# Merging the second combine into the first expert stretch of a fused attention and two-mixture kernel

## What is computed

```python
y = x + attention(rmsnorm(x) * scale1)            # linear attention, 16 heads, chunks of 64
z = y + moe(rmsnorm(y) * scale2)                  # 8 experts, top 2, gelu, capacity 1280 rows each
x = layernorm(x + z)                              # the second combine, see below
x = layernorm(x + ffn(layernorm(x) * gamma + beta))   # 8 experts, top 2, silu(g) * u, capacity 1280
```

## Time and profile before

| | us |
|---|---|
| median of three runs | 1545.46 |
| the profiled execution | 1548.21 |
| its span, first to last instruction | 1546.3 |
| PE busy | 1461.0 (94%) |
| DVE busy | 1011.2 (65%) |
| ACT busy | 727.1 (47%) |
| POOL busy | 746.5 (48%) |
| mean granted clock of PE | 0.963 of full |

### The profile page before, as it was taken

One profiled execution on the slowest core, in us unless ns is written; L12 is line 12 of the kernel. 1 busy time (PEld: TensorE's weight loads), 2 busy tenths in 40 slices (PEclk: granted clock), 3 DMA queues, 4 the chain that ended last, 5 costly groups with the idle time before them and its releaser, 6 DMA issues. The chain is left out here.

```text
span 1546.3 us, 36023 instructions
## 1 busy us (share of the span) xinstructions
PE 1461.0 (94%) x11755; PEld 1419.0 (92%) x11755; DVE 1011.2 (65%) x2768; ACT 727.1 (47%) x1735; POOL 746.5 (48%) x749
## 2 busy tenths in 40 slices
PE   8999984999999999999949999999999999999993
PEld 7888864999999999999938999999999999999993
DVE  6999976667667667666565656565565655566455
ACT  4767653555455445545543334343433433344333
POOL 3677652566566566655523344433444334433433
PEclk9999995999999999999968999999999999999996
DMA  7122123244234243342613132413132131411117
GB/s 257 42 70 56 56 73 108 58 102 103 42 96 102 48 96 93 51 130 35 192 50 109 27 111 33 116 29 109 28 108 42 27 109 29 115 34 28 28 24 228
DMA packets 64547, 123.41 MB, mean 80 GB/s; under 512 B 14304, under 2 KB 52832, under 8 KB 61792
## 3 DMA queue, kind: packets, MB, share of 16 engines
q0 software_dynamic: 36416, 46.58, 18.4%
q1 hardware_dynamic: 28064, 76.02, 13.7%
HBM read 79.66 MB, written 42.90 MB: 79 GB/s over the span
## 5 line engine op out<-in xcount | busy, mean ns | idle before, releaser
L972 POOL DMA_INDIRECT acc<-ysb,IDX x160 | 258.8, 1617 | 132.4 <-ACT ysb L1074 66.3
L1111 DVE TENSOR_TENSOR E_hraw<-E_sg,bank 128x256 f32<-128x256 f32 x320 | 134.5, 420 | 282.7 <-ACT E_sg L1042 214.2
L965 POOL DMA_INDIRECT E_mg<-meta,IDX x160 | 151.0, 943 | 335.6 <-DVE E_gate L1095 308.4
L1166 PE MATMUL bank<-E_xT,ws 128*128 128x256 f32 x960 | 272.2, 284 | 5.1 <-DVE E_xT L1086 5.0
L1167 PE MATMUL bank<-E_xT,ws 128*128 128x256 f32 x960 | 271.5, 283 | 0.0
L1168 PE MATMUL bank<-E_xT,ws 128*128 128x256 f32 x960 | 271.3, 283 | 0.0
L1122 DVE TENSOR_TENSOR E_hT<-E_hraw,E_hT 128x256 fp32r<-128x256 f32 x640 | 259.9, 416 | 0.0
L1118 DVE CAST E_hT<-E_hraw 128x256 fp32r<-128x256 f32 x640 | 208.0, 325 | 62.1 <-ACT E_hraw L1045 40.2
L1042 ACT ACTIVATE E_sg<-bank 128x256 f32<-128x256 f32 x320 | 121.6, 384 | 256.3 <-PE bank L1168 243.4
L1166 PEld LDWEIGHTS bank<-E_xT,ws 128*128 128x128 f32 x960 | 183.0, 191 | 6.3 <-issue 5.8
L1166 PE MATMUL bank<-ws,E_hT 128*128 128x256 f32 x640 | 183.8, 287 | 0.0
(11 more groups left out here) (207 smaller groups left out, 3940.6 us busy)
## 6 DMA issues: line engine op xcount, KB each, us to landing
wraw<-in_w_ffn SPq DMA_DIRECT2D x8, 3072.0 KB, 10.7
wraw<-in_w_moe SPq DMA_DIRECT2D x8, 2048.0 KB, 13.0
X<-acc SPq DMA_DIRECT2D x16, 512.0 KB, 5.4
acc<-x SPq DMA_DIRECT2D x32, 128.0 KB, 1.7
xn<-xn SPq DMA_DIRECT2D x32, 128.0 KB, 1.7
acc<-X POOLq DMA_DIRECT2D x4, 1024.0 KB, 8.3
acc<-X SPq DMA_DIRECT2D x8, 512.0 KB, 2.7
out<-C_xo SPq DMA_DIRECT2D x8, 512.0 KB, 5.6
```

Of the source, the lines that this page charges most:

```text
L965: nc.gpsimd.indirect_dma_start(out=mg[:, j, :], out_offset=None, in_=meta_dram, in_offset=at_slots(u, j)).then_inc(s_gm, 16)
L972: nc.gpsimd.indirect_dma_start(out=acc_dram, out_offset=at_slots(u, j), in_=ysb[:, j, :], in_offset=None, compute_op=ALU.add).then_inc(s_y ...
L1111: V.tensor_tensor(hraw[:, f % RING, :], sg[:, f % RING, :], bank[f % RING][:, UW:2 * UW], ALU.mult).then_inc(s_hm, 1)
L1166: nc.tensor.matmul(out, wh, mh, start=first, stop=False)
```

## The change

The combine of stage 4 becomes the tail of E1's block, and the routing a block of its own. In detail:

- The 20 spare products at E1's end go. PE turns the eight early tiles as soon as the last unit's bias add is done, then issues three spare products, then goes on with tile 8. One spare product per tile stays, as before.
- Group 2 is loaded in three pieces: tile 8, tile 9, tiles 10 and 11 (`SPANS`).
- POOL normalises, and SP stores, groups 0 to 5 in the first block; groups 6 and 7 (`LATE` = 2) follow in the routing's block, behind the routing's two constants on POOL.
- ACT's warm-up of the root, which held its table load, goes. The turned tiles go into `b2`, which has the same eight places of 256 columns as `aT` had. `META` moves to a buffer of the whole program.

```diff
@@ SPANS
+SPANS = [(g * G, (g + 1) * G) for g in range(HEAD)] + [(8, 9), (9, 10), (10, 12)]     # HEAD * G = 8
+SPANS += [(g * G, (g + 1) * G) for g in range(HEAD + 1, GROUPS)]
@@ expert_phase, tail=C for E1
             for g in range(HEAD):
                 ...
+            if tail:
+                sp.wait_ge(s_ys, 16 * UT * UNITS)
+                tail.sync(sp)
...
+            if tail:
+                tail.pool(pool, range(GROUPS - LATE))
...
+            if tail:
+                tail.act(act, b2)
...
+            if tail:
+                tail.vector(dve)
...
-            if not glu:
-                keep_busy(nc, bank[7], ws[0], 20)
+            if tail:
+                pe.wait_ge(s_sg, UNITS * NF + RING)
+                pe.wait_ge(s_ye, UNITS * UT + UT)
+                tail.tensor(pe, b2)
@@ class Between, from between_phase; vector() as it was
+    def aT(self, b2, n):
+        return b2[:, n % (2 * G), :].rearrange("p (k t) -> p k t", k=KD)
+    def store(self, sp, groups):
+        for g in groups:
+            t = slice(g * G, (g + 1) * G)
+            sp.wait_ge(self.s_x2, (g + 1) * G)
+            sp.dma_start(by_partition(self.io["acc2"])[:, t, :], self.X[:, t, :]).then_inc(self.s_sa, 16)
+    def sync(self, sp):
+        for i in range(HEAD, len(SPANS)):
+            t = slice(*SPANS[i])
+            sp.dma_start(self.X[:, t, :], by_partition(self.io["acc1"])[:, t, :]).then_inc(self.s_ldx[i], 16)
+        self.store(sp, range(GROUPS - LATE))
...
-            nc.scalar.activation(warm[:, :], eps, ACT.Sqrt)
...
         for n in range(NT + 3):
+            if n == HEAD * G:
+                keep_busy(nc, self.bank[7], self.ws0, 3)
             if n < NT:
                 turn(n)
             keep_busy(nc, self.bank[7], self.ws0, 1)
             if n >= 3:
                 logits(n - 3)
@@ second_routing_phase, a block of its own
+            C.store(sp, range(GROUPS - LATE, GROUPS))
             R.store(sp)
+            sp.wait_ge(C.s_sa, 16 * GROUPS)
...
             R.constants(pool)
+            C.pool(pool, range(GROUPS - LATE, GROUPS))
```

More of the change, by code:

```diff
@@ L1224, in sem @@
             return ctx.enter_context(nc.semaphore(f"C1_{name}"))
[L1226 to L1237, removed]
@@ new lines, in __init__ @@
+        self.wrg, self.fold, self.ws0 = wrg, fold, ws0
+        self.bias = sb("bias", [P, NT, E])
+        self.st = sb("st", [P, 2, G, 6])
+        self.mv = sb("mv", [P, 2, G, 2])
+        self.sd = sb("sd", [P, 2, G, 2])
+        self.rs = sb("rs", [P, NT])
+        self.nb = sb("nb", [P, NT])
+        self.s_ldx = s_head + [sem(f"ldx{g}") for g in range(HEAD, len(SPANS))]
+        self.s_bs, self.s_mv, self.s_sd, self.s_rs, self.s_nb = map(sem, ("bs", "mv", "sd", "rs", "nb"))
+        self.s_x2, self.s_tr, self.s_aT, self.s_rt, self.s_sa, self.s_base = map(sem, ("x2", "tr", "aT", "rt", "sa", "base"))
@@ new lines, in sync, with pool @@
+    def sync(self, sp):
[3 more added lines that the diff above has]
+        self.store(sp, range(GROUPS - LATE))
+    def pool(self, pool, groups):
+        X, rs, nb = self.X, self.rs, self.nb
+        for g in groups:
+            pool.wait_ge(self.s_nb, g + 1)
+            for n in range(g * G, (g + 1) * G):
+                pool.wait_ge(self.s_tr, n + 1)
+                self.nc.gpsimd.tensor_scalar(X[:, n, :], X[:, n, :], rs[:, n:n + 1], nb[:, n:n + 1], ALU.mult, ALU.add).then_inc(self.s_x2, 1)
@@ new lines, in act @@
+    def act(self, act, b2):
+        nc, sd, mv = self.nc, self.sd, self.mv
+        eps, eps2 = self.cst[:, C_EPS:C_EPS + 1], self.cst[:, C_EPS + 1:C_EPS + 2]
+        for g in range(GROUPS):
+            if g >= 2:
+                act.wait_ge(self.s_rt, (g - 1) * G)
+            for n in range(g * G, (g + 1) * G):
+                act.wait_ge(self.s_tr, n + 1)
+                nc.scalar.activation(self.aT(b2, n), self.turned(n), ACT.Copy).then_inc(self.s_aT, 1)
+            act.wait_ge(self.s_mv, (g + 1) * G)
+            if g >= 2:
+                act.wait_ge(self.s_rs, 2 * (g - 1))
+            nc.scalar.activation(sd[:, g % 2, :, 0], mv[:, g % 2, :, 1], ACT.Sqrt, bias=eps).then_inc(self.s_sd, 1)
+            nc.scalar.activation(sd[:, g % 2, :, 1], mv[:, g % 2, :, 1], ACT.Sqrt, bias=eps2, scale=1.0 + EPS).then_inc(self.s_sd, 1)
@@ new lines, in tensor, with turn, logits @@
+    def tensor(self, pe, b2):
+        nc, ident = self.nc, self.cst[:, C_ID:C_ID + P]
+        def turn(n):
+            self.loaded(pe, n)
+            if n >= 5:
+                pe.wait_ge(self.s_aT, n - 4)
+            for k in range(KD):
+                ins = nc.tensor.transpose(self.turned(n)[:, k, :], self.X[:, n, k * P:(k + 1) * P], ident)
+            ins.then_inc(self.s_tr, 1)
+        def logits(n):
+            pe.wait_ge(self.s_aT, n + 1)
+            for k in range(KD):
+                ins = nc.tensor.matmul(self.bank[0][:, D + n * E:D + (n + 1) * E], self.aT(b2, n)[:, k, :], self.wrg[:, k, :],
+                                       start=(k == 0), stop=(k == KD - 1))
+            ins.then_inc(self.s_rt, 1)
+        for n in range(NT + 3):
+            if n == HEAD * G:
+                keep_busy(nc, self.bank[7], self.ws0, 3)
+            if n < NT:
+                turn(n)
+            keep_busy(nc, self.bank[7], self.ws0, 1)
+            if n >= 3:
+                logits(n - 3)
@@ L1296, in _ @@
         def _(dve):
[L1297 to L1328, removed]
-            V.tensor_tensor(bias[:, :, :], bias[:, :, :], fold[:, 0, :].unsqueeze(1).to_broadcast([P, NT, E]), ALU.add).then_inc(s_base, 1)
-            dve.wait_ge(s_base, 2)
-            dve.wait_ge(s_rt, NT)
             R.select(dve)
```

113 lines of the change are left out of this document (50 added, 63 removed).

## The result

The changed kernel took 1537.94 us in the median of five runs (1535.95 to 1541.09), the kernel before 1545.46; the ratio is 0.9959, 95% interval 0.9948 to 0.9970, so 6.3 us less (4.6 to 8.0); the two medians lie 7.5 apart. Forecast were 1543.6 and a range down to 1541.8, with 0.19 for a gain of over 0.2%. The sign was right, but the gain was three times that forecast, and outside the range.

What follows compares the result with a forecast made beforehand. PE was taken to bound the combine's end, with routing waiting for it and the loads for POOL's last add. Terms -2.9 + 0.3 + 0.7 = -1.9 us from 1545.46 gave 1543.6, range 1541.8 to 1546.1.

Steps and rivals of the forecast that it cites:

- Early tiles: Start of the combine: PE goes from the last product to tile 0 at 745.4, 4.4 us earlier than before.
- ACT's table load at nothing: Early tiles of the combine: ACT's 1.28 us table load for the root, after four evictions, costs nothing.
- The load of tile 8 is what is late next, -2.9: Combine: tile 8's 128 KB load takes 2.6 us, so PE turns it at 752.55 instead of 755.46.
- The meeting of the engines, +0.3: Between last logits and first routing operation: the engines' meeting, hidden before, now lies on the path, +0.3 us.
- POOL's last two groups in the routing, +0.7: Routing: POOL working beside DVE slows DVE's operations on two SBUF tensors, +0.7 us.
- The clock falls: Combine loop, rival: PE's idle waits halve its clock, making it slower, about 1563 us; chance 0.05.
- The step that failed: Closing sum over the combine and routing: -1.9 us in all, with the turned tiles' move of memory changing no wait.

Runs made afterwards that it cites:

- e7: The changed kernel with LATE = 0, so that POOL normalises all eight groups before the routing; 1542.95 us in one execution.
- e8: The changed kernel without the three spare products ahead of tile 8; 1560.24 us.
- e1: The kernel before with two unused buffers giving the expert stages' large buffers the change's addresses, nothing else changed; 1544.01 us, ratio 0.9970 to the kernel before.
- e2: The changed kernel with META2 and the combine's buffers at SBUF's other end, so expert buffers keep their old addresses; 1544.13 us, ratio 0.9974 to the kernel before.
- e3: The changed kernel itself, run again word for word on another chip; 1543.29 us, ratio 0.9964 to the kernel before.
- e4: The changed kernel with weights and rows all shifted alike by 32 bytes per partition; 1543.91 us, ratio 0.9968 to the kernel before.
- e5: The changed kernel with the experts' rows and hidden values 64 bytes further from the weights; 1537.72 us in one execution.
- e12: The changed kernel with tiles 8 to 11 loaded in one piece of 512 KB; 1537.63 us in one run.

## Why the prediction was wrong

- **Early tiles**: right. Tile 0 was due 0.7 us ahead of the last add and came at 0.72.
- **ACT's table load at nothing**: right, no wait of PE on an eviction; the load took the 1.28 us of the earlier trace rows.
- **The load of tile 8 is what is late next, -2.9**: right in kind; 2.37 us from issue (746.92) to turn (749.29) where 2.6 + 0.05 were put: -3.1. It starts 3.90 us after the add was issued, forecast 3.79. Over all ten profiles with this piece, issue to turn took 2.36 to 2.81 us, so the forecast size was right and the first profile is at its lower end. The estimate by the Trainium skill (DMA: Bandwidth & Descriptors, Anatomy of one DMA), 2.3 us for 128 KB, is that lower end; the page has its formula from transfers issued by GpSimd, while SyncE issued this one.
- **The meeting of the engines, +0.3**: 772.42 - 771.97 = 0.45 after the last logits, against 0.10 before; +0.35.
- **POOL's last two groups in the routing, +0.7**: e7 gives 0.75. Of it only 0.4 is new, since the kernel before paid the first part already (0.54 beside POOL), which I did not take off. The Trainium skill (GPSIMD Engine Reference, Specifications) has GpSimd contend with VectorE's operations that read two SBUF inputs, or that run in a two-port mode. The trace agrees for the first: products of two SBUF tensors took up to 0.66 for 0.42, and reductions stayed at 0.42. The one-input clamp at 773.36 was stretched too, 0.38 against 0.29 in e7; whether it is of the second kind no run here shows.
- R_sel to IDX 0.34 shorter, in every kernel with the merged block. Not forecast; VectorE no longer stands idle for 0.25 us there; the cause is open.
- **The clock falls**, 0.05: it did not, and e8 shows that it was a real branch with the right price. The forecast wait of 0.75 us was 0.42, and up to 0.71 in the other profiles.
- **The step that failed** is the one that closed the sum: it ran over the block alone, and of memory it said only that the double buffer for turned tiles "moves to the bias tensor's memory with the same eight places, so no wait changes". The tensors made ahead of the weights in the diff were costed at nothing, without a word. They moved every operand of the expert layers, where PE is the bound for all of 1180 us. What was put at 0 measured 4.6 us (2.6 to 6.7) alone in e1; the merged block alone, forecast 1.9, measured 4.0 (2.5 to 5.4) in e2. In the profiles the addresses are worth 3.4 to 3.7 us in the experts of the first layer that read `ws0`, and 0.9 to 1.0 in the second layer, on both chips; the block's own place is worth 2.7, which is 1.9 with -3.1 for -2.9, +0.4 for +0.7 and the 0.3 not forecast. The whole first layer moved by 5.3 us on one chip and by 1.5 to 3 on the other (e2 against e1, e3 and e4), the rest being mostly waits in the last expert that don't go with the distance.
- **Luck**: that the addresses moved to faster distances is chance. In e5, with 64 bytes more, the first layer took 458.37 us where e7 on the same chip, with the distances of the change, took 456.87.

That it pays to move buffers could not have been read from the trace of before. That they moved could be read from the diff: 1% of PE's time there is six times the forecast gain. A risk of unknown size belonged in the range, with both signs.

## What to carry to other kernels

Where a diff makes, drops or reorders buffers, list how the addresses of the operands of the bounding engine move, however far from the edit; with PE bound for 1180 us, 0.5% of pace outweighs the 2.7 us of the whole edit. Compare the number of products started in a full stretch between the two traces before explaining anything else. Where PE bounds in such products, try offsets between the operands by a pad of 16 to 48 elements: here distances of 64 were worth five times the whole gain of the change, and distances of 0 cost 10 us against the kernel before.

## What the runs showed of the hardware

- A 128x256 product with fp32r operands, weights reloaded each time, goes at 0.1134 to 0.1200 us from start to start at a granted clock of 1.00, by the distance modulo 256 bytes from the held operand to the one that passes through. Whole kernel: 1553.97 us where rows and weights lie 0 apart, 1509 to 1512 where they lie 64 apart. A common shift of both by 32 bytes did nothing (e4).
- At distances 64 and 192 the pace has two levels in one execution, 0.1134 and 0.1178, held through a round of a unit; at 160 they are 0.1174 and 0.1187.
- PE idle for 1.49 us without dense passes ahead: granted clock 0.50 for 85 us (e8). Idle for 1.67 us behind three passes: 1.00 up to the last logits (e12). One execution each.
- A load of 128 KB of rows from HBM, the first of a series in its queue, could be used 2.36 to 2.81 us after its issue (ten executions), one of 512 KB in its place 3.70 (e12).
- Left open: why pace follows that distance, what picks the level at 64, 160 and 192, and what holds ACT for 2.4 us in the last expert on one chip.
